# Masks of two pairs loaded once and spread by shuffles, masking moved to GpSimd, and the plain products put behind all weight units

## The reference

```python
def reference(x, cond_8, L0_cond_weight, L0_cond_mask, L0_cond_bias):
    def _L0_cond_ref(x, y, weight, mask, bias):
        masked_w = weight * mask[None, :, :]                 # (8, 256, 256)
        w_bot = jnp.einsum('bg,got->bot', y, masked_w)       # (32, 256, 256)
        return jnp.einsum('bnt,bot->bno', x, w_bot) + bias
    return x + _L0_cond_ref(x, cond_8, L0_cond_weight, L0_cond_mask, L0_cond_bias)
# x (32, 256, 256), cond_8 (32, 8), weight (8, 256, 256), mask (256, 256), bias (256,), all fp32
```

## Time and profile before

| | |
|---|---|
| time, median of 3 runs | 66.73 us |
| the 3 runs | 66.37, 66.73, 66.96 us |
| profiled execution, first to last instruction (span) | 65.5 us |
| around the span, to the median | 1.2 us |
| TensorE busy | 58.8 us (90%) |
| VectorE, ScalarE, GpSimd busy | 48.1, 47.9, 7.0 us |
| granted TensorE clock, mean | 0.999 |

### The profile page before, as it was taken

One profiled execution on the slowest core, in us unless ns is written; L12 is line 12 of the kernel. 1 busy time (PEld: TensorE's weight loads), 2 busy tenths in 40 slices (PEclk: granted clock), 3 DMA queues, 4 the chain that ended last, 5 costly groups with the idle time before them and its releaser, 6 DMA issues.

```text
span 65.5 us, 1501 instructions
## 1 busy us (share of the span) xinstructions
PE 58.8 (90%) x645; PEld 54.3 (83%) x645; DVE 48.1 (73%) x36; ACT 47.9 (73%) x40; POOL 7.0 (11%) x17
## 2 busy tenths in 40 slices
PE   2997188999999999999999999999999999999910
PEld 1266087977888899999999999999999999999900
DVE  2109809999957989999999999989999992250200
ACT  2506609799889999999999799999869986005520
POOL 5500299900000000000000000000000000000000
PEclk9999999999999999999999999999999999999999
DMA  0999999999998157954999999999999229918393
GB/s 0 260 373 306 352 412 422 407 434 428 420 410 340 60 85 255 408 215 198 245 285 225 400 451 420 403 441 423 398 413 425 93 100 408 398 63 325 158 372 116
DMA packets 5334, 20.21 MB, mean 309 GB/s; under 512 B 592, under 2 KB 1104, under 8 KB 4432
## 3 DMA queue, kind: packets, MB, share of 16 engines
q1 hardware_dynamic: 5040, 19.89, 79.6%
q10 hardware_dynamic: 288, 0.23, 1.1%
HBM read 11.73 MB, written 8.39 MB: 307 GB/s over the span
## 4 chain that ended last, share of the span: by engine, by line
PE 79%; DMA 9%; ACT 4%; SPq 2%; issue 1%
PE slots L433 20%; PE slots L431 20%; PE slots L432 20%; PE slots L451 11%; DMA weights<-in_first 9%; PE slots L332 6%; ACT w_raw L534 3%; PE slots L326 2%; ACT weights L563 1%; SPq L230 1%; SPq L222 1%; SPq L229 1%
## 5 line engine op out<-in xcount | busy, mean ns | idle before, releaser
L431 PE MATMUL slots<-x_hi,w_hi 128*128 128x256 f32 x112 | 31.4, 280 | 0.0
L432 PE MATMUL slots<-x_lo,w_hi 128*128 128x256 f32 x112 | 31.2, 279 | 0.0
L433 PE MATMUL slots<-x_hi,w_lo 128*128 128x256 f32 x112 | 31.2, 279 | 0.0
L431 PEld LDWEIGHTS slots<-x_hi,w_hi 128*128 128x128 f32 x112 | 21.1, 188 | 0.0
L432 PEld LDWEIGHTS slots<-x_lo,w_hi 128*128 128x128 f32 x112 | 21.1, 188 | 0.0
L433 PEld LDWEIGHTS slots<-x_hi,w_lo 128*128 128x128 f32 x112 | 21.1, 188 | 0.0
L589 DVE TENSOR_TENSOR x_lo<-x_ring,x_hi 128x2048 fp32r<-128x2048 f32 (+1 forms) x8 | 16.1, 2022 | 0.5 <-ACT x_hi L491 0.5
L491 ACT CAST x_hi<-x_ring 128x2048 fp32r<-128x2048 f32 (+1 forms) x8 | 13.5, 1694 | 1.3 <-DMA x_ring<-in_x 1.3
L511 ACT ACTIVATE weights<-slots,smalls 128x1024 f32<-128x1024 f32 x10 | 10.8, 1112 | 4.7 <-PE slots L433 4.7
L598 DVE TENSOR_TENSOR w_lo<-w_raw,w_hi 128x2048 fp32r<-128x2048 f32 x6 | 13.7, 2288 | 0.2 <-ACT w_hi L499 0.2
L499 ACT CAST w_hi<-w_raw 128x2048 fp32r<-128x2048 f32 x6 | 11.5, 1909 | 0.0
(11 more groups left out here) (25 smaller groups left out, 19.3 us busy)
## 6 DMA issues: line engine op xcount, KB each, us to landing
out<-weights SPq DMA_DIRECT2D x15, 512.0 KB, 4.7
x_ring<-in_x SPq DMA_DIRECT2D x7, 1024.0 KB, 9.6
x_ring<-in_first SPq DMA_DIRECT2D x6, 512.0 KB, 7.2
weights<-in_first SPq DMA_DIRECT2D x4, 256.0 KB, 6.6
out<-weights SPq DMA_DIRECT2D x1, 256.0 KB, 2.4
out<-weights SPq DMA_DIRECT2D x1, 128.0 KB, 2.3
out<-weights ACTq DMA_DIRECT2D x1, 128.0 KB, 2.1
smalls<-in_small ACTq DMA_DIRECT2D x1, 97.0 KB, 3.1
```

What stands on the lines that cost most here:

```text
L431: nc.tensor.matmul(dst, wh, xh, start=(k == 0), stop=False)
L432: nc.tensor.matmul(dst, wh, xl, start=False, stop=False)
L433: last = nc.tensor.matmul(dst, wl, xh, start=False, stop=(k == KC - 1))
```

## The change

Five edits, all in stage 1 and at its seam with stage 2:

1. The mask rows of pairs 0 and 1 are no longer sent with the weights. They come once, as `compact` (128x256, 128 KB), issued by ScalarE's queue ahead of `smalls`: of each eight rows that share a mask row, four hold a quarter (256 columns) of the two pairs' masks.
2. VectorE spreads them: four stream shuffles, each copying one quarter to all eight rows of each group, into the last slot of `x_ring` (`mask_half(c)`).
3. GpSimd multiplies the masks for all four pairs, in place in `weights`; VectorE has no `mask_pair` any more.
4. A pair's two sides come in one transfer (`pair`, 512 KB); pairs 2 and 3 still bring full masks (`mask`, 256 KB). `x` of group 0 is one transfer of 1 MB in the common layout.
5. `EARLY` is gone: units 2 to 7 in a row, then all sixteen plain matmuls; ScalarE's and VectorE's pieces for group 1 (now two, not three) stand behind all units, and group 0's first result is one 128x1024 step.

```diff
-EARLY = 6
-ORDER = (("other", 0), ("masked", 0), ("masked", 1), ("other", 1), ("off", 0), ("masked", 2), ("other", 2), ("x", 0),
-         ("masked", 3), ("other", 3), ("x", 1))
+ORDER = (("other", 0), ("masked", 0), ("pair", 1), ("off", 0), ("pair", 2), ("mask", 2), ("pair", 3), ("mask", 3), ("x", 0))
...
+        mask_rows = x_ring[:, XS - 1, :]
+        def mask_half(c):
+            return mask_rows[:, c * COMPACT:(c + 1) * COMPACT]
...
-        pieces = ((0, NB // 2, 0), (NB // 2, NB, 0), (0, NB, 1))
+        pieces = ((0, NB, 0), (0, NB, 1))
...
-            return slots[:, (1, 0, 3, 2)[(2 * g + h) % SLOTS], :]
+            return slots[:, (3, 0, 1, 2)[(2 * g + h) % SLOTS], :]
...
-            sp.dma_start(staged(0), in_order("masked", 0)).then_inc(masked_loaded[0], 16)
+            sp.dma_start(blocks[:, 0, :], in_order("masked", 0)).then_inc(first_masked_loaded, 16)
             load_pair(1)
...
+            sp.dma_start(x_ring[:, 0, :], in_order("x", 0)).then_inc(x_loaded[0], 16)
             load_group(1)
-            sp.wait_ge(masked_by_dve, 2)
-            sp.wait_ge(masked_by_pool, 2)
-            load_group(XS - 2)
-            sp.wait_ge(masked_by_pool, 2 * (PAIRS - 2))
-            sp.wait_ge(masked_by_dve, 4)
+            load_group(2)
+            sp.wait_ge(masked_by_pool, 2 * PAIRS)
             load_group(XS - 1)
...
+            def mask_pair(j):
+                pool.wait_ge(first_masked_loaded if j == 0 else pair_loaded[j - 1], 16)
+                if j >= SPREAD:
+                    pool.wait_ge(mask_loaded[j - SPREAD], 16)
+                for i in range(2):
+                    if j < SPREAD:
+                        pool.wait_ge(mask_spread, 2 * j + i + 1)
+                    nc.gpsimd.tensor_tensor(blocks[:, 2 * j, half_of(i)], blocks[:, 2 * j, half_of(i)],
+                                            mask_half(2 * j + i), ALU.mult).then_inc(masked_by_pool, 1)
...
             weigh_first_pair()
-            for u in range(SIDES, EARLY):
+            for u in range(SIDES, UNITS):
                 weigh_unit(u)
-            pe.wait_ge(raw_by_act, EARLY - 1)
+            pe.wait_ge(raw_by_act, UNITS - 1)
             pe.wait_ge(raw_by_dve, UNITS // HO)
             pe.wait_ge(raw_masked, 1)
-            pe.wait_ge(half_x_loaded, 16)
-            multiply_first(early, 0, 0, NB // 2).then_inc(early_ready, 1)
-            for u in range(EARLY, UNITS):
-                weigh_unit(u)
-            pe.wait_ge(raw_by_act, UNITS - 1)
             pe.wait_ge(x_loaded[0], 16)
-            multiply_first(product(0, 0)[:, BANK:SLOT], 0, NB // 2, NB).then_inc(products_ready, 1)
+            multiply_first(0)
             pe.wait_ge(raw_by_act, UNITS)
             pe.wait_ge(raw_by_dve, UNITS)
-            multiply_first(product(0, 1), 1, 0, NB).then_inc(products_ready, 1)
+            multiply_first(1)
...
         def _(act):
+            act.dma_start(compact[:], mask).then_inc(compact_loaded, 16)
             act.dma_start(smalls[:], small).then_inc(smalls_loaded, 16)
...
-            mask_pair(0)
+            dve.wait_ge(compact_loaded, 16)
+            for c in range(CHUNKS):
+                nc.vector.stream_shuffle(mask_half(c), compact[:], [G * (i // G) + c for i in range(ROWS)]).then_inc(mask_spread, 1)
```

150 lines of the change are left out of this document (63 added, 87 removed).

## The result

| | before | changed |
|---|---|---|
| time, median (lowest to highest) | 66.76 us (66.37 to 66.96, 4 runs) | 67.55 us (67.29 to 67.94, 4 runs) |
| ratio, 95% interval | | 1.0147 [1.0092, 1.0202] |
| spans | 64.3 in the new profile below | 65.4, 65.9, 65.6, 65.3 us |
| time less span | 1.74 to 1.97 us over the 68 recorded runs, mostly 1.8 | 2.07, 2.04, 2.03, 1.99 us |

The change made the kernel **1.5% slower**. The forecast was 66.1 us, and 67.55 lies outside its range too. The profiled execution of the changed kernel took 67.47 us. In this part, T is again the time at which VectorE starts on unit 2. "Time less span" is how much longer the execution took than the stretch from its first to its last instruction.

What follows compares the result with a forecast made beforehand. TensorE was taken to bound the kernel, groups 1 to 7 filling it unchanged, so only group 1's start mattered. Span 65.5 less 0.6 us gives 64.9, plus 1.2 around it 66.1 us; range 65.3 to 67.1.

Steps and rivals of the forecast that it cites:

- Span 65.5 - 0.6 = 64.9; with the 1.2 us around it 66.1: Whole kernel: profiled span less the gain, plus time outside the span, gives the forecast time of 66.1 us.
- the gain of 0.6: End of stage 1: group 1 would start at 22.6 us instead of 23.20, 0.6 us earlier.
- smalls 0.4 later at 4.3: Head: with compact first in ScalarE's queue at about 3.95, smalls would land at 4.3 us instead of 3.87.
- pair 1 and its mask: Start of unit 2: pair 1 landing at 7.1 us, then GpSimd's masking, would set T at 9.26.
- the forecast's own 0.69: Start of unit 2: VectorE starts 0.69 us behind the end of GpSimd's masking of pair 1.
- their removal costs nothing because that gap closes as well: Before the products: early products only filled TensorE's wait for unit 6; the reordering alone gains about 0.1 us.
- T + 6.03: End of the units: TensorE ends unit 7 and could start the plain products 6.03 us after T, at 15.3.
- the shuffles: Head, VectorE: four shuffles spread the compact masks, taken at 0.40 us each and ending at 5.6.
- rival (a): Stage 1 loads: the stream binds; late x gives 66.9 us, late mask 2 gives 66.5; chance 0.25 shared with another rival.
- the tie at unit 4: Unit 4: pair 2's masking would be ready at 11.70 us, just as VectorE arrives at 11.69.
- the lock: Head: if shuffles locked the shared SBUF port, GpSimd's pair 0 would end at 7.0; sum stays 66.1, cover falls to 0.4.
- Rival (c): Head: shuffles ahead of VectorE's unit 0 become the bound, up to 68.1 us; chance 0.08 together with a still later load.

Runs made afterwards that it cites:

- before_again: The kernel before, unaltered, profiled once more; 66.06 us (one run), span 64.3.
- smalls_first: The changed kernel with smalls issued ahead of compact on ScalarE's queue; 67.88 us, ratio 1.019.
- reorder_only: Part 5 of the change alone on the kernel before, with pair 3 masked on GpSimd and its loads ahead of x; 67.41 us, ratio 1.010.
- shift12: The changed kernel with 12 thin matmuls (16 columns) behind the four identities, ahead of the wait for smalls; 68.44 us (one run).
- changed_again: The changed kernel, unaltered, measured and profiled again; 68.15 us, ratio 1.029.
- keep_busy: The changed kernel with three 512-column matmuls on zeros behind the identities, where TensorE waits for smalls; 67.94 us, ratio 1.022.
- before_shuffle: The kernel before with one unused 128x32 stream shuffle on VectorE while it is idle; 66.29 us, ratio 0.997.
- shift32: The changed kernel with 32 thin matmuls (16 columns) behind the four identities, ahead of the wait for smalls; 67.90 us, ratio 1.022.

## Why the prediction was wrong

**The base.** "Span 65.5 - 0.6 = 64.9; with the 1.2 us around it 66.1" is the step that failed first. 65.5 was a long execution and 1.2 was got by taking its span from the median of other executions. The changed kernel's own span came out 0.6 above the forecast (median 65.5, against 64.9), and 2.05 us lie outside it. Of the miss of 1.45 us (67.55 against 66.1), 0.85 is this term (0.65 that was already there before, 0.2 new) and 0.6 is span. The same error hid the sign: the gain of 0.6 was reckoned from T = 9.81 and a span of 65.5, but the median span of the kernel before is 64.8. A forecast span of 64.9 was, unseen, a forecast of no gain, and against an execution like before_again (64.3) of a loss.

**The smalls.** "smalls 0.4 later at 4.3" was mis-sized: 1.0 to 1.6 us later than the 3.87 of before (4.9 to 5.5 in the runs with that order of issue). T came out as said, 9.19 against 9.26, but for another reason: the chain from smalls, not pair 1 and its mask. Both near 9.2 was chance: pair 1 landed at 6.6 and GpSimd had its mask done at 8.1, which by the forecast's own 0.69 gives 8.8. In smalls_first T is 8.99 with half the head at half speed and the masks later; what it would be with neither fault was not measured.

**The early products.** "their removal costs nothing because that gap closes as well" failed. This is the 0.6 us of span: products were to start at T + 6.03 and started at T + 6.83, 0.8 later, of which a T earlier by 0.07 and products shorter by 0.1 gave 0.2 back. The forecast priced the wait for unit 6 and not the hole that the early products covered; reorder_only and shift12 show that the hole belongs to a place in the list. It costs 0.3 to 1.0 us on the path (T + 6.54 to 7.16 with it, T + 6.12 to 6.27 without). Without it the changed kernel's products would have started at 15.3 to 15.5 by these distances, an estimate; 15.3 was said.

**The head's speed** appears nowhere in the prediction. Where it strikes all of the head, T comes 4.9 to 5.1 us after the first weighing, against 3.8 in the three profiles with full speed (changed, changed_again, keep_busy): 1.0 to 1.3 us. The profiles of the changed kernel itself do not have it, so it is no part of their 67.47 and 67.44 us.

**Right were** the shuffles (0.43 us, and one started every 0.34; the forecast took 0.40), GpSimd's pairs (1.42), the loads (earlier than said by 0.5 to 1.1; rival (a) did not come up), the tie at unit 4, which cost nothing (unit 6 waited for the hole instead), 32 records of products in 7.17 us, and 39.2 us behind them. The page "VectorE: DVE Perf Modes" of the Trainium skill, section "The perf-mode tier table", gave an estimate of 0.30 a shuffle; the trace has 0.34, a little nearer to it than to the 0.40 taken. Of the lock in the Trainium skill's page "SBUF — State Buffer", section "SBUF: two separate sides", the shuffles show no sign: in changed_again GpSimd's four halves took 2.94 us (0.74 each, 0.71 alone) from 4.79 on, with VectorE's shuffles running until 5.5. Rival (c), slower because the head becomes the bound, was right in its place and wrong in its mechanism: not the shuffles but the transfer ahead of smalls.

**Open:** what sets off the half speed (smalls_first, before_shuffle and reorder_only have it after a wait as short as in the kernel before; neither the landing time nor the wait alone sorts the profiles), when the packet of instructions is fetched (reading 32 records further moved it by more than one step), and the 0.2 us outside the span, which come with parts 1 to 4 but not with the array, the first shuffle or a late last packet.

## What to carry to other kernels

Before a sum is made on a profiled execution, see whether it is a typical one: compare its span and its first landings with the times, and get the time outside the span from the same execution. A transfer put in front of a small one that an engine's first work waits for can cost far more than its bytes: here 128 KB cost 1.0 to 1.6 us, where the 410 KB a us of the profile before would give 0.3, an estimate. Work that seems only to fill a wait may cover a stop that belongs to a place in the list as well; moving it away can open a hole that no semaphore explains, and adding or removing records ahead of that place tells such a hole from one that belongs to the work.

## What the runs showed of the hardware

- TensorE stops at a fixed place of its list if it comes there too soon after a 16 KB packet of instructions began: in eleven profiles it went on 2.3 to 2.6 us after that (11.46 to 13.96 in the changed kernel, 11.82 to 14.17 in reorder_only, 11.37 to 13.88 in changed_again). The hole was 0.09 to 0.82 us. In shift32 and in before_again, where it came there some 3.1 us after the packet, there was none.
- TensorE's loads of 32x128 took 29 ns each or 55, in executions of near equal kernels with the same wait, while the granted clock of that stretch was shown as 1.00. 32 thin matmuls (29 ns each) ahead of them did not hold the speed.
- Loads of the same kernel land up to 1.2 us apart from one execution to the next (7.11 and 8.29 for the other side of pair 1), and T went with it (8.51 and 9.81).
